# Graph network on one core: TensorE's pick loop written out, query windows of eight rows for seven groups, one table split on GpSimd

## What is computed

```python
# attention layer, three times (L1 twice, L2 once)
alpha = jnp.sum(q[dst] * k[src], axis=-1) * SCALE            # L2: + edge_bias[edge_type]
m = jax.ops.segment_max(alpha, dst, num_segments=N)
a = jnp.exp(alpha - m[dst]);  denom = jax.ops.segment_sum(a, dst, num_segments=N)
out = jax.ops.segment_sum(v[src] * (a / denom[dst])[:, :, None], dst, num_segments=N)
# maximum layer, twice (L3)
agg = jax.ops.segment_max(h[src], dst, num_segments=N)
x = (h + agg) @ W + b
```

## Time and profile before

| | |
|---|---|
| median of 3 runs | 6553.22 us (6550.06 to 6576.66) |
| the profiled execution's own time | 6574.14 us |
| its span | 6572.5 us |
| busy: DVE / POOL / ACT / PE | 4554.9 / 3883.7 / 2521.1 / 2285.5 us |
| granted clock of PE over the span | 0.667 |

### The profile page before, as it was taken

One profiled execution on the slowest core, in us unless ns is written; L12 is line 12 of the kernel. 1 busy time (PEld: TensorE's weight loads), 2 busy tenths in 40 slices (PEclk: granted clock), 3 DMA queues, 4 the chain that ended last, 5 costly groups with the idle time before them and its releaser, 6 DMA issues.

```text
span 6572.5 us, 44667 instructions
## 1 busy us (share of the span) xinstructions
PE 2285.5 (35%) x14635; PEld 1383.5 (21%) x14635; DVE 4554.9 (69%) x5458; ACT 2521.1 (38%) x3136; POOL 3883.7 (59%) x3861
## 2 busy tenths in 40 slices
PE   3997500000010000000100000035888783877876
PEld 2775300000000000000100000013444441444443
DVE  7978587777767777777687777774666653656654
ACT  2340144444323444443244433433444442444443
POOL 1001277777747777775577777716666555655664
PEclk7998755555555555555555555557999895988987
DMA  1233454444435444443454444412333332333332
GB/s 63 81 121 137 136 162 158 149 149 148 155 114 171 159 151 149 149 154 126 143 168 149 150 153 150 146 46 86 111 103 111 103 100 75 111 101 101 103 101 88
DMA packets 262138, 826.79 MB, mean 126 GB/s; under 512 B 72362, under 2 KB 109274, under 8 KB 258115
## 3 DMA queue, kind: packets, MB, share of 16 engines
q0 software_dynamic: 165280, 426.11, 22.6%
q1 hardware_dynamic: 96679, 398.78, 16.8%
HBM read 492.30 MB, written 341.93 MB: 127 GB/s over the span
## 4 chain that ended last, share of the span: by engine, by line
POOL 38%; PE 27%; issue 21%; DVE 7%; ACT 2%; another core or an unknown queue 2%; DMA 1%; SPq 0%; DVEq 0%; POOLq 0%; ACTq 0%
POOL arena L2327 37%; PE pair_ps L1874 20%; PE pair_ps L1971 4%; DVE outs L925 1%; PE banks_ps L1949 1%; ACT outs L1712 1%; PE banks_ps L1840 1%; DVE outs L1003 1%; DVE work L1153 0%; PE pair_ps L1883 0%; DVE bn_st L703 0%; PE pair_ps L1987 0%; ACT arena L1690 0%; POOL H L2327 0%
## 5 line engine op out<-in xcount | busy, mean ns | idle before, releaser
L2327 POOL DMA_INDIRECT arena<-table,src_i x3596 | 3633.4, 1010 | 1766.9 <-issue 1251.5
L1852 PE MATMUL pair_ps<-ident,tails 128*128 128x128 f32 x9 | 2.7, 439 | 3366.7 <-DVE tails L1260 2242.1
L1874 PE MATMUL pair_ps<-bias,arena 128*128 128x384 bf16 x4050 | 790.9, 345 | 312.9 <-issue 261.7
L1098 DVE TENSOR_TENSOR pair_ps<-pair_ps,arena 128x1792 f32<-128x1792 f32 x168 | 341.4, 2032 | 711.2 <-DMA arena<-table,src_i 481.9
L1874 PE MATMUL pair_ps<-work,arena 128*128 128x384 bf16 x4050 | 754.2, 337 | 162.3 <-issue 161.0
L1003 DVE TENSOR_TENSOR_SCAN outs<-arena,banks_ps 128x1920 f32<-128x1920 f32 x112 | 465.1, 4153 | 496.4 <-ACT banks_ps L1698 471.6
L1852 PEld LDWEIGHTS pair_ps<-ident,tails 128*128 128x128 f32 x9 | 1.5, 213 | 3369.0 <-DVE tails L1260 2243.8
L1153 DVE TENSOR_TENSOR_SCAN work<-work,banks_ps 128x1920 f32<-128x1920 f32 x168 | 697.6, 4153 | 5.8
L1578 ACT ACTIVATE LD<-DE 128x112 f32<-128x112 f32 x168 | 49.8, 296 | 1423.4 <-issue 647.6
L1874 PEld LDWEIGHTS pair_ps<-bias,arena 128*128 128x128 bf16 x4050 | 405.3, 101 | 679.2 <-issue 465.9
L1598 ACT COPY outs<-work 128x1792 f32<-128x1792 f32 x171 | 541.8, 3170 | 0.0
(11 more groups left out here) (320 smaller groups left out, 4382.8 us busy)
## 6 DMA issues: line engine op xcount, KB each, us to landing
rows_att<-outs SPq DMA_DIRECT2D x165, 1008.0 KB
rows_plain<-outs SPq DMA_DIRECT2D x110, 896.0 KB
arena<-table,src_i POOLq DMA_INDIRECT x3596
kept_counts<-arena SPq DMA_DIRECT2D x15, 2000.0 KB, 6.4
bias<-sources SPq DMA_DIRECT2D x108, 192.0 KB
arena<-kept_counts SPq DMA_DIRECT2D x10, 2000.0 KB, 8.3
outs<-kept_counts SPq DMA_DIRECT2D x5, 2000.0 KB, 7.7
qchunks<-qtable SPq DMA_DIRECT2D x3, 3136.0 KB
```

Source lines behind the costliest of these rows:

```text
L1098: chain(v.tensor_tensor(prod, prod, ring[:, s, :, 0:D], ALU.mult))
L1874: ins = pe.matmul(picked_ps[g % 2], parts3[:, a, t, :], hots_made[g % 2][:, :, t, :], start=t == a == 0, stop=t == NB - 1 and a == 2)
L2327: pool.indirect_dma_start(dst, None, tab, bass.IndirectOffsetOnAxis(ap=idx, axis=0))\
```

## The change

It has three parts, cut to their core:

```diff
-SHARE = 4
-CHUNK = 4
-QROWS = 2 * CHUNK
-CHUNKS = 784
+SHARE = 7
+QROWS = SHARE + 1
 SPANS = GROUPS // SHARE
-MOVES = SHARE + 1
+MOVES = SHARE - 1
...
-            firsts = dst_i[:, :].rearrange("p (a t) -> p a t", a=SPANS)[:, :, 0]
-            step(v.tensor_single_scalar(chunk_i[:, :], firsts, CHUNK.bit_length() - 1, ALU.arith_shift_right))
-            for i in range(2):
-                step(v.tensor_single_scalar(chunk_bit[:, i, :], firsts, 2 >> i, ALU.bitwise_and))
-            step(v.tensor_scalar(chunk_on[:, :, :], chunk_bit[:, :, :], 0.0, None, ALU.is_gt))
...
             def move_on(k, g):
                 if g % SHARE == 0:
-                    moved(2, SHARE + 2, chunk_on[:, 0, span:span + 1], at - 1)
-                    moved(1, SHARE + 1, chunk_on[:, 1, span:span + 1], at)
-                else:
-                    moved(1, SHARE + 1 - g % SHARE, next_on[:, g:g + 1], at)
+                    return
+                rows3, left, n = window[:, g // SHARE % 2, :, :], QROWS - g % SHARE, window_moved(k, g)
+                if n > 1:
+                    v.wait_ge(s_moved, n - 1)
+                v.copy_predicated(rows3[:, 0:left, :], next_on[:, g:g + 1].unsqueeze(2).to_broadcast([P, left, D]),
+                                  rows3[:, 1:1 + left, :]).then_inc(s_moved, 1)
...
-            for stage, b in in_stages("graph", 1):
+            for stage, b in in_stages("graph"):
...
-                elif stage == 10:
-                    take_block_apart(5, b)
...
-            def pick(k, g, it=None):
-                await_count(s_onehot, made_group(k, g) + 1, 2, it)
+            def pick(k, g):
+                pe.wait_ge(s_onehot, made_group(k, g) + 1)
...
             def pick_rows(k):
-                pe.wait_ge(s_vec, MARK[f"parts{k}"])
-                first = PICK_FROM
-                for g in range(first, first + 2):
+                if k == 5:
+                    pe.wait_ge(s_apart, 5 * NBLK)
+                else:
+                    pe.wait_ge(s_vec, MARK[f"parts{k}"])
+                for g in range(PICK_FROM, GROUPS):
                     pick(k, g)
-                with pe.Fori(0, (GROUPS - first) // 2 - 1) as it:
-                    for g in range(first + 2, first + 4):
-                        pick(k, g, it)
                 turn_picked(k, GROUPS - 1)
...
-                pairs = bass.AP(qtable[k].tensor, 0, [[CHUNK * D, CHUNKS], [1, QROWS * D]])
-                sp.dma_start(qchunks[k], pairs).then_inc(s_chunks, 16)
...
             def fetch_window(k, span):
-                fetch(window[:, span % 2, :, :].rearrange("p r f -> p (r f)"), qchunks[k],
-                      chunk_i[:, span:span + 1], s_window[span % 2])
+                fetch(window[:, span % 2, :, :].rearrange("p r f -> p (r f)"), qtable[k],
+                      dst_i[:, span * SHARE * GROUP:span * SHARE * GROUP + 1], s_window[span % 2])
...
                 with pool.Else():
+                    fetch_window(k, 0)
                     for g in range(GROUPS):
...
-                        if g == 0:
-                            pool.wait_ge(s_chunks, 16 * (att_number(k) + 1))
-                            fetch_window(k, 0)
...
+            def take_block_apart(b):
+                b0, b1 = BLOCKS[b]
+                pool.wait_ge(s_norm, 3 * NBLK + b + 1)
+                rows3 = H[:, b0:b1, :]
+                rest = work[:, REST_AT:REST_AT + (b1 - b0) * D].rearrange("p (i f) -> p i f", f=D)
+                if b:
+                    pool.wait_ge(s_apart, 5 * b)
+                pool.tensor_copy(parts3[:, 0, b0:b1, :], rows3).then_inc(s_apart, 1)
+                pool.wait_ge(s_apart, 5 * b + 1)
+                pool.tensor_tensor(rest, rows3, parts3[:, 0, b0:b1, :], ALU.subtract).then_inc(s_apart, 1)
+                pool.wait_ge(s_apart, 5 * b + 2)
+                pool.tensor_copy(parts3[:, 1, b0:b1, :], rest).then_inc(s_apart, 1)
+                pool.wait_ge(s_apart, 5 * b + 3)
+                pool.tensor_tensor(rest, rest, parts3[:, 1, b0:b1, :], ALU.subtract).then_inc(s_apart, 1)
+                pool.wait_ge(s_apart, 5 * b + 4)
+                pool.tensor_copy(parts3[:, 2, b0:b1, :], rest).then_inc(s_apart, 1)
...
             for k in range(2, PASSES):
                 run_pass(k)
                 fetch_nodes(k)
+                if k == 4:
+                    for b in range(NBLK):
+                        take_block_apart(b)
```

More of the change, by code:

```diff
@@ L205, in gnn_kernel @@
         qtable = {k: dram(f"qtable{k}", [NODES, D]) for k in range(PASSES) if KINDS[k] == ATT}
-        qchunks = {k: dram(f"qchunks{k}", [CHUNKS, QROWS * D]) for k in qtable}
         rows = {MAX: dram("rows_plain", [EPAD, D]), ATT: dram("rows_att", [EPAD, AW])}
@@ L531, in gnn_kernel @@
         s_pick = sem("rows_picked")
+        s_apart = sem("table_parts_laid")
         s_whole = sem("picked_rows_laid")
@@ L1027, in take_block_apart @@
                 b0, b1 = BLOCKS[b]
-                if k in (0, 5):
-                    v.wait_ge(s_norm, (3 * NBLK if k else 0) + b + 1)
+                if k == 0:
+                    v.wait_ge(s_norm, b + 1)
                 elif k == 1:
@@ L1603, in lay_fences, with last_max @@
                          flags[:, bass.ds(g, 1), :].to_broadcast([P, HEADS, GROUP + 1]))
-            def last_max(s, b, g):
-                ins = act.copy(UA[:, b, 1, :, 0], MS[:, (s - 1) % RING, :, GROUP])
-                if isinstance(g, int) and g == 0:
-                    ins.then_inc(s_begun, 1)
+            def last_max(s, b):
+                act.copy(UA[:, b, 1, :, 0], MS[:, (s - 1) % RING, :, GROUP])
             def lay_queries(k, s, b, g):
@@ L1623, in lay_far @@
             def lay_far(k, s, b, g):
-                last_max(s, b, g)
+                last_max(s, b)
                 lay_fences(b, g)
@@ L1857, in carry_turns @@
                 ins.then_inc(s_cout, 1)
-            def await_count(semaphore, value, each, it):
-                if it is None:
-                    pe.wait_ge(semaphore, value)
-                else:
-                    pe.wait_ge(semaphore, it * each + value)
-                    pe.nop(nofuse=True)
-            def pick(k, g, it=None):
-                await_count(s_onehot, made_group(k, g) + 1, 2, it)
+            def pick(k, g):
+                pe.wait_ge(s_onehot, made_group(k, g) + 1)
                 for t in range(NB):
                     if t == TURN_AT and g > PICK_FROM:
-                        turn_picked(k, g - 1, it)
+                        turn_picked(k, g - 1)
                     for a in range(3):
@@ L1876, in pick, with turn_picked @@
                 ins.then_inc(s_pick, 1)
-            def turn_picked(k, g, it=None):
-                await_count(s_whole, made_group(k, g) + 1, 2, it)
-                await_count(s_spread, scanned(k, g - 2), 2, it)
+            def turn_picked(k, g):
+                pe.wait_ge(s_whole, made_group(k, g) + 1)
+                pe.wait_ge(s_spread, scanned(k, g - 2))
                 for u in range(MAKE):
@@ L2242, in store_kvq @@
                     sp.dma_start(block_of(qtable[k], b), queries).then_inc(done, 16)
-                for b in range(NBLK - QBUF, NBLK):
-                    sp.wait_ge(s_kvq[b % QBUF], kvq_count(k, b))
-                pairs = bass.AP(qtable[k].tensor, 0, [[CHUNK * D, CHUNKS], [1, QROWS * D]])
-                sp.dma_start(qchunks[k], pairs).then_inc(s_chunks, 16)
             def store_linear(k, name):
```

21 lines of the change are left out of this document (4 added, 17 removed).

## The result

The changed kernel is slightly slower: 6577.6 us (median of 17 runs, 6552.7 to 6595.2) against 6556.2 (17 runs, 6539.5 to 6576.7), a ratio of 1.0027 with a 95% interval of 1.0016 to 1.0038. On another chip it was 1.0017 (1.0005 to 1.0029). (The ratios aren't the quotients of the medians. Where a cost is given "by the ratio", it is the ratio's distance from 1 times the median of before; it differs by up to 7 us from the difference of the medians, here 18 against 21.) That is inside the 0.5% that a single measurement of this kernel can tell, but with so many runs both intervals lie above 1. I had forecast 6518.

A forecast was written before the change was run, and what follows sets the result against it. POOL's issuing bounds passes 2 to 4; in the maximum passes, POOL's burst plus a late PE signal set a group's length. Savings 23.5 + 2 + 10 + 0 = 35.5 us give 6518 us for the median, range 6465 to 6558.

The forecast's parts named there:

- Windows on POOL: Attention passes: 6 fewer window instructions on POOL a pass, 18 in all at 1.30 us, saving 23.5 us.
- The data's pace: Rival, attention passes: POOL's pace comes from data moved, so the windows save only a few us: 6541; chance 0.10.
- Chunk table: Attention passes: the earlier first window only lets DVE wait longer for rows, as POOL sets the pace: 0 us.
- DVE's relief: Attention passes: 12.8 us less DVE work a pass shortens POOL's gathers slightly: 2 us of a possible 3.5.
- Table apart: Before pass 5: splitting the table on POOL instead of DVE starts the gathers earlier, 14.2 - 4 = 10 us.
- that comes 14.2 us earlier: Before pass 5: the last block's normalisation comes 14.2 us earlier, with five of six block splits off DVE.
- Loop written out: PE's loop in the maximum passes: POOL's burst and the late signal set the group's length, so 0 us.
- Picks free: Rival: fewer PE instructions let the transposes' signal out before POOL's burst and long waits vanish: about 6470; chance 0.15.
- Code fetches hold PE: Rival: 61 more code blocks fetched while POOL bursts hold PE up; at 1.2 us each 73 us, 6591; chance 0.10.
- Slow split: Rival: POOL slow at the split, 8 us a block, or getting in DVE's way; the 10 us go, 6528; chance 0.15.
- The rule on taken branches: PE's loop: by the skill, branches out of the two-page window force a fetch; written out wins one per turn; not summed.
- The signs I had named: Wrong if an attention pass keeps its length, POOL's waits in passes 5 and 6 change over 30 us, or PE gaps appear.

The follow-up runs named there:

- windows: Kernel before with only the windows changed (eight rows for seven groups, no chunk table): 6526.5 us, ratio 0.9964.
- unroll: Kernel before with only PE's loop in the maximum passes written out: 6596.0 us, ratio 1.0057.
- after_2: The changed kernel run again on another chip, against the kernel before: 6574.7 us, ratio 1.0017.
- before_3: Kernel before, unchanged, for a second profile on a chip where it takes near 6550 us: passes 5 and 6 took 980.0 and 993.0 us.
- unroll_paced: Kernel before with PE's loop written out, plus two semaphore instructions a group: 5852.1 us, ratio 1.0000; repeated on another chip, 6572.6 us, ratio 1.0020.
- before_again: Kernel before, unchanged, profiled on a chip of the quicker kind, where its median was 5851.7 us.

## Why the prediction was wrong

*Windows on POOL, 23.5 us: right.* 7.6, 7.5 and 8.1 us a pass, 23.2 in sum; 23.6 in the timed runs of windows. The data's pace, the rival, is out: the mean gather stayed at 1032 ns, and the gaps between gathers are 0.33 us as before ((262.7 + 49.9 - 47.7) / 791; 47.7 is the one ahead of the first).

*Chunk table, 0: right.* ACT's wait shrank by 17.2 us and DVE's wait for rows grew by 66 us.

*DVE's relief, 2 us: wrong by its size.* The rows show 1033 and 1032 ns a gather, with DVE 12.8 us less busy: 1 us a pass at most, within rounding, and the windows account for all of the 23.2.

*Table apart, 10 us: wrong.* POOL's side was sized well: 0.61 us a cast and 1.15 a subtraction, 4.4 us a block with its gaps against my 4.7, and a first gather 4.2 us later relative to the last normalisation against my 3 to 4. By the Trainium skill ("GPSIMD Engine Reference", section 3), which has a two-input addition 1.96 times slower on GpSimd, my estimate for the subtraction was 1.36 us; the trace has 1.153 against DVE's 0.692, a factor of 1.67. The step that failed is "that comes 14.2 us earlier": it came 6.8 us earlier, as DVE's other instructions got longer beside POOL's. So 2.6 us were left of 10. I had that only as a rival ("by getting in DVE's way") with the gain as its stake, whereas the part costs 17 to 29 us in the timed runs, and 49 on chip C. Those I can't place. Pass 5 of the four profiles with the split on POOL and the old windows has 7 to 11 bursts of 22, against 5 to 7 without the split, some 10 us at 3.55 each; but their passes 5 and 6 together take 1953 to 1979 us, and the two profiles of before 1961 and 1973. So no loss shows in the passes, and elsewhere only the 4 us between the attention passes do. On chip C, where POOL never stops within a maximum pass, five of six runs took 5890 to 5907 us, and the profiled one, with 5858, was the sixth.

*Loop written out, 0: wrong, and it is the step on which the sign turned.* The term was set to 0 with "The group's length is set by POOL's burst and the late signal", "not by the count of PE's instructions"; alone it cost 37 us (24 to 52). The sentence holds for a single burst. It left out that the signal is at times early, and that this costs 4 to 5 us each time instead of saving. I read the long waits of the earlier trace rows, 55 us a pass above the usual 3.12, as a thing that could only get better, though I had before me 46 waits at the 51 places between bursts behind the opening: the missing five were the double bursts. In the profiles of unroll, the changed kernel and after_2, five of the six passes have 9 to 13 of them (2 to 11 in the ten passes with the loop and without the split; the two ranges overlap), and the written-out form costs 37 us alone and 11 to 18 beside the others. In the profiled pair the changed kernel's 25 bursts of 22 against 16 make 32 us at 3.55 each, near the 37 that its two passes grew by. That is this pair. It doesn't carry over to the loop alone, whose profile has fewer bursts of 22 (14) than either profile of before, nor to after_2 (18, as before_3). So what the loop's form costs is shown by the timed runs, and its cause is open: it isn't the code fetches, whose number I had right (61, measured 62) and which delay no group in a single burst, and PE's pace as such isn't shown to be it. With two more semaphore instructions a group (unroll_paced) some two thirds of the loss were gone, but on another chip.

*The rivals.* Picks free: no, the picks themselves keep their pace, 349 and 342 ns a matmul in place of 345 and 337. Code fetches hold PE (slower): the right side for a wrong reason. Slow split: 6528, the nearest of them for the term, far from the result. None had what the profile of the changed kernel shows: a signal that comes early and costs time by it.

*The rule on taken branches.* The prediction sets the loop against the Trainium skill ("Runtime: NRT & Kernel Launch", instruction fetch mechanics) and says that the trace disagrees. That reading was too quick. The rule is for a branch that leaves the window of two pages; the trace shows that 700 us of looping brought no block, and no row shows whether this loop ever leaves its window. So the trace neither refutes the rule nor gives the written-out form a fetch to win.

*The signs I had named.* POOL's waits changed by less than 30 us together (-5 in pass 5, 213.9 to 190.9 in pass 6); that sign missed the loss, which in this profile showed in POOL's busy time. I should have asked for the length of the passes.

The range, 6465 to 6558, was built from terms that were each sized on one execution, 18 us above its median. Passes 5 and 6 of two executions of the same kernel (on two chips) differ by 15 and 2 us in the profiles (965.3 and 980.0; 995.4 and 993.0), its runs by 40. With such a scatter the range had to reach further above no change. Had I priced the 16 double bursts of the profile before, twice as many would have been 57 us at 3.55 each. That the profiled pair differs by 21.0 us and the medians by 21.4 is luck: both executions lie 18 us above their medians.

## What to carry to other kernels

Where an engine waits for a slot of a ring in a steady rhythm, count its waits against the groups before you cost a change at nothing: groups without a wait are a second rhythm, and the mix changes from one run to the next (25 and 18 bursts of 22 in two profiles of the changed kernel). Work moved from DVE to POOL isn't free for DVE; price it with DVE's remaining instructions lengthened wherever the two meet. And test bundled changes part by part: here one part earned 19 to 40 us on each of the four chips where it ran, and two that were to be free or a gain ate it.

## What the hardware showed that I had not expected

**Two kinds of chips.** The same program took 6574 us on one chip (profile before) and 5840 on another (before_again). The attention passes took 1090 and 1006 us, with mean gathers of 1033 and 957 ns; the maximum passes 965 to 995 and 784. PE's picks over the whole run, in the profile of before and of before_again:

```profile
L1874 PE MATMUL pair_ps<-bias,arena 128*128 128x384 bf16 x4050 | 790.9, 345 | 312.9 <-issue 261.7
```
```profile
L1874 PE MATMUL pair_ps<-bias,arena 128*128 128x384 bf16 x4050 | 687.4, 330 | 49.4 <-DVE bias L1020 49.4
```

The 261.7 us of idle without a cause are gone from this row. So the hold that POOL's gathers have on PE belongs to the chip or its surroundings, not to the program; what differs there no profile shows. Four of the six chips were of the slower kind.

**PE under POOL's long bursts.** In the opening of the changed pass 5, POOL starts at 4411.12 and PE issues freely until 4431; then one matmul in 1.4 to 3.5 us, mostly 2.8, until POOL's burst of 61 is over (4488.2), and full pace again from 4497.

**Gathers of 6.47 us** beside DVE's one-hots, on chips of the slower kind alone; before_again has none above 1.5 us in its maximum passes.
